# Five instead of four strips per head on VectorE, head sums on GpSimd, memory units later in the head

## The reference, cut to what matters

```python
scores = jnp.einsum('bsqhd,bthd->bqhst', qh, kh) * scale
probs = jax.nn.softmax(scores, axis=-1)
a_dot = jnp.einsum('bqhst,bthd->bsqhd', probs, vh)
a_mem = sigma_q @ memory / (sigma_q @ memory_norm)
out = a_dot * (1.0 - w) + a_mem * w          # x = x + out
x_qdq = quantised_to_fp8(_layernorm(x))      # x = x + x_qdq @ w.T
```

## Time and profile before

| what | value |
|---|---|
| median of three runs | 1942.49 us |
| the profiled execution | 1942.58 us, span 1940.5 us |
| PE busy | 1863.9 us, 96% |
| PEld busy | 1162.0 us, 60% |
| DVE busy | 1409.9 us, 73% |
| ACT busy | 1833.6 us, 94% |
| POOL busy | 107.2 us, 6% |
| granted TensorE clock | 1.000 |
| chain that ended last | ACT 76%, PE 21%, issue 2%, DVE 1% |

### The profile page before, as it was taken

One profiled execution on the slowest core, in us unless ns is written; L12 is line 12 of the kernel. 1 busy time (PEld: TensorE's weight loads), 2 busy tenths in 40 slices (PEclk: granted clock), 3 DMA queues, 4 the chain that ended last, 5 costly groups with the idle time before them and its releaser, 6 DMA issues.

```text
span 1940.5 us, 115379 instructions
## 1 busy us (share of the span) xinstructions
PE 1863.9 (96%) x54988; PEld 1162.0 (60%) x54996; DVE 1409.9 (73%) x1833; ACT 1833.6 (94%) x1596; POOL 107.2 (6%) x150
## 2 busy tenths in 40 slices
PE   8999999999999999999999999999999999999998
PEld 7885555556565555555555555555655555555555
DVE  6675777777777777787777777777777777777755
ACT  5556999999999999999999999999999999999997
POOL 5541000000000000000000000000000000000000
PEclk9999999999999999999999999999999999999999
DMA  6654111121112211222112211212112211222111
GB/s 220 201 187 153 54 54 40 45 57 45 54 41 56 78 49 42 56 58 64 47 49 56 78 47 44 57 46 76 44 53 57 78 50 41 56 50 72 43 47 46
DMA packets 131327, 130.38 MB, mean 67 GB/s; under 512 B 30451, under 2 KB 106455, under 8 KB 130855
## 3 DMA queue, kind: packets, MB, share of 16 engines
q1 hardware_dynamic: 129847, 121.15, 21.2%
q10 hardware_dynamic: 1008, 1.84, 0.3%
HBM read 86.96 MB, written 32.24 MB: 61 GB/s over the span
## 4 chain that ended last, share of the span: by engine, by line
ACT 76%; PE 21%; issue 2%; DVE 1%; POOL 0%; DMA 0%; ACTq 0%; DVEq 0%; POOLq 0%
ACT pool L865 74%; PE ps L1153 8%; PE ps L945 6%; PE ps L1028 4%; ACT pool L872 1%; PE ps L1200 1%; PE ps L918 1%; DMA resid<-in_x 0%; PE ps L984 0%; POOL q_sq L727 0%; PE ps L909 0%; POOL xn L704 0%; PE ps L926 0%; DVE v_tiles L1608 0%; DVE v_tiles L1610 0%
## 5 line engine op out<-in xcount | busy, mean ns | idle before, releaser
L865 ACT ACTIVATE pool<-ps 128x1536 f32<-128x1536 f32 (+1 forms) x1388 | 1710.1, 1413 | 17.0 <-PE ps L1028 14.7
L1153 PE MATMUL ps<-pool,v_st 64*32 64x128 f32 (+2 forms) x35744 | 1398.3, 357 | 14.7 <-issue 13.7
L1153 PEld LDWEIGHTS ps<-pool,v_st 64*32 64x32 f32 x35744 | 854.5, 106 | 210.0 <-issue 54.3
L1028 PE MATMUL ps<-q_st,k_st 51*32 51x512 f16 x16128 | 903.6, 381 | 49.0 <-ACT pool L865 11.6
L1028 PEld LDWEIGHTS ps<-q_st,k_st 51*32 51x32 f16 x16128 | 246.0, 89 | 474.3 <-ACT pool L865 427.5
L1593 DVE TENSOR_SCALAR late<-ps 128x512 int32<-128x512 f32 x248 | 171.6, 692 | 212.5 <-PE ps L1028 212.5
L1608 DVE SCALAR_TENSOR_TENSOR v_tiles<-late 128x2048 f32<-128x2048 f32 x62 | 142.1, 2293 | 148.1 <-PE ps L1153 144.7
L1612 DVE SCALAR_TENSOR_TENSOR pool<-v_tiles,late 128x2048 f32<-128x2048 f32 x62 | 142.1, 2292 | 2.1
L1610 DVE SCALAR_TENSOR_TENSOR v_tiles<-v_tiles,late 128x2048 f32<-128x2048 f32 x62 | 142.1, 2292 | 2.1
L1603 DVE SCALAR_TENSOR_TENSOR late<-late 128x2048 f32<-128x2048 f32 x62 | 141.6, 2285 | 0.0
L747 POOL TENSOR_TENSOR rstd<-var_eps,minus_half 128x1 f32<-128x1 f32 x32 | 23.0, 720 | 1696.8 <-DVE var_eps L1672 1696.8
(11 more groups left out here) (169 smaller groups left out, 955.1 us busy)
## 6 DMA issues: line engine op xcount, KB each, us to landing
v_st<-v_aug SPq DMA_DIRECT2D x64, 256.0 KB, 3.5
q_st<-q_aug SPq DMA_DIRECT2D x127, 128.0 KB
k_st<-k_aug SPq DMA_DIRECT2D x127, 128.0 KB
sigma_kept<-y_out SPq DMA_DIRECT2D x32, 256.0 KB, 2.0
q_aug<-parts SPq DMA_DIRECT2D x32, 256.0 KB, 2.7
wqT<-sigma_kept SPq DMA_DIRECT2D x32, 256.0 KB, 3.8
q_st<-q_aug SPq DMA_DIRECT2D x127, 64.0 KB
k_st<-k_aug SPq DMA_DIRECT2D x127, 64.0 KB
```

Of the source, the lines that this page charges most:

```text
L865: act.activation(probs[:, u % HELD, 0:UNITS[u].width * CH], scored(u).rearrange("p a b -> p (a b)"), ACT.Exp, bias=LIFT, scale=EXP_UNIT / ...
L1028: return pe.matmul(ps[VW * c:VW * c + VW, bank, :], k_st[RT * r:RT * r + AUG, n % 2, keys:keys + VW], q_st[RT * r:RT * r + AUG, n % 2, q * ...
L1153: last = pe.matmul(acc[r][VW * c:VW * c + VW, :].rearrange("v (i s) -> v i s", s=VW)[:, places, :], v_st[rows, n % 2, j, :], by_place[rows ...
```

## The change

Each of the heads 1 to 62 gets a fifth late strip, the last strip of the key tile before the last. ScalarE keeps 22 units per head, with one 3-wide unit fewer and one 2-wide more. In the even head the two memory units move from places 0 and 2 to 3 and 5. The late strips are weighed as a piece of four and a piece of one, in units 15 and 16 of even heads and 13 and 14 of odd ones. The polynomial is worked out in place in the pool, and its last step (`finish_late`) moves to the next head: first in even heads, behind the output of the tile in odd ones. Two of the four steps that join a head's sums move to GpSimd, except where the head before was the last of its chunk. The third strip's row tile alternates with every unit. Head 0 has 25 units for the same 64 strips, 24 before.

```diff
+LATE_STRIPS = tuple(range(HEAD_STRIPS - QG, HEAD_STRIPS)) + (HEAD_STRIPS - QG - 1,)
+LATE = len(LATE_STRIPS)
-UNITS_OF_HEAD = (["2memory", "3", "2memory"] + ["3"] * 7 + ["2late"] * 4 + ["3"] * 8,
-                 ["3", "3", "2product", "3", "2spare", "3", "3"] + ["2late"] * 4 + ["3"] * 11)
+EVEN_HEAD = ["3", "3", "3", "2memory", "3", "2memory"] + ["3"] * 3 + ["2late"] * LATE + ["3"] * 8
+ODD_HEAD = ["3", "3", "2product", "3", "2spare", "3", "3"] + ["2late"] * LATE + ["3"] * 10
-WEIGHED_LATER = ((0, 1, 2), (0, 1, 2, 3, 9))
-WEIGH_LATE_AT = 14
+WEIGHED_LATER = ((0, 1, 2), (0, 1, 2, 3))
+LATE_PIECES = ((0, 4), (4, 1))
+WEIGH_LATE_AT = (15, 13)
...
+            for n in range(1, LAST_HEAD):
...
+                if n % 2 == 0 and n >= HEADS:
+                    tile = (n - HEADS) // 2
+                    pool_e.wait_ge(f_eps, tile + 1)
+                    pool_e.tensor_tensor(rstd[:, 0, 0:1], var_eps[:, 0:1], minus_half[:, 0:1], ALU.pow).then_inc(f_rstd, 1)
+                    pool_e.wait_ge(f_rstd, tile + 1)
+                if n % HEADS != 0:
+                    add_sums(n - 1)
...
-                    last = strip_scores(THIRD_BANK[u % SLOTS], n, strip, (c // 2 + u // 2) % ROW_TILES, c)
+                    last = strip_scores(THIRD_BANK[u % SLOTS], n, strip, (c // 2 + u) % ROW_TILES, c)
...
+            def finish_late(n):
+                dve.wait_ge(late_step, n * CHAIN_STEPS)
+                dve.scalar_tensor_tensor(late_probs, late_probs, POWER[3], late_x, ALU.add, ALU.mult).then_inc(late_ready, 1)
...
             def head(n):
                 g, h = divmod(n, HEADS)
-                if n % 2 == 0:
-                    add_memory(n)
+                if n % 2 == 0 and n > 0:
+                    finish_late(n)
                 if n > 0:
                     take_sums(n - 1)
+                for unit in extras(n, "product", "weight") * (n % 2):
...
                 if n % 2 == 0:
+                    if n > 0:
+                        dve.wait_ge(sums_added, n - 1)
+                    add_memory(n)
                     add_memory(n + 1)
+                else:
+                    finish_late(n)
                 if n > 0:
-                    add_sums(n - 1)
+                    sum_halves(n - 1)
+                    if h == 0:
+                        add_sums(n - 1)
```

More of the change, by code:

```diff
@@ L99, in extra_of, with forms_of_head @@
     return None, 0
+def forms_of_head(n):
+    if n == 0:
+        return ["2"] * EARLY_UNITS + EVEN_HEAD[:-1] + ["2", "2"]
+    return (EVEN_HEAD, ODD_HEAD)[n % 2]
 def units_of(n):
     units, strip, names = [], 0, []
-    for form in ["2"] * EARLY_UNITS * (n == 0) + UNITS_OF_HEAD[n % 2]:
+    for form in forms_of_head(n):
         width, name = int(form[0]), form[1:]
@@ L748, in rstd_of_tiles, with add_sums @@
                     pool_e.wait_ge(f_rstd, i + 1)
[L750 to L755, removed]
+            def add_sums(n):
+                g, h = divmod(n, HEADS)
+                pool_e.wait_ge(rden_ready, n + 1)
+                pool_e.tensor_tensor(head_out[:, :, :, 0:DH], head_out[:, :, :, 0:DH],
+                                     rden[:, :, :].unsqueeze(3).to_broadcast([P, QG, TPC, DH]), ALU.mult)\
+                    .then_inc(head_out_ready, 1)
+                pool_e.wait_ge(head_out_ready, n + 1)
+                cols = resid[:, g * TPC:(g + 1) * TPC, :].rearrange("p t (q f) -> p q t f", q=QG)[:, :, :, h * DH:(h + 1) * DH]
+                pool_e.tensor_tensor(cols, cols, head_out[:, :, :, 0:DH], ALU.add).then_inc(sums_added, 1)
+            for n in range(1, LAST_HEAD):
+                if n == LAST_HEAD - 1:
+                    pool_e.wait_ge(scores_ready, EXP_BASE[LAST_HEAD - 1])
+                    pool_e.memset(q_st[:, 1, :].bitcast(F32), 0.0).then_inc(last_cleared, 1)
+                    pool_e.wait_ge(last_cleared, 1)
+                if n % 2 == 0 and n >= HEADS:
[5 more added lines that the diff above has]
+                    add_sums(n - 1)
+            rstd_of_tiles((NG - 1) * TPC, NT)
             pool_e.wait_ge(xq_ready, NT)
@@ L1174, in weigh_unit, with weigh_late @@
                     last.then_inc(pv_done, 1)
-            def weigh_late(n, x):
+            def weigh_late(n, piece):
+                first, strips = LATE_PIECES[piece]
                 pe.wait_ge(late_ready, n)
-                last = weigh(n, LATE_TILE, late_probs[:, x * CH:x * CH + CH], x, 1)
-                if x == LATE - 1:
+                j, q = divmod(LATE_STRIPS[first], QG)
+                last = weigh(n, j, late_probs[:, first * CH:(first + strips) * CH], q, strips)
+                if piece == len(LATE_PIECES) - 1:
                     last.then_inc(late_weighed, 1)
@@ L1233, in head @@
                         weigh_unit(weighed)
-                    x = u - EXP_BASE[n] - WEIGH_LATE_AT
-                    if n > 0 and 0 <= x < LATE:
-                        weigh_late(n, x)
+                    piece = u - EXP_BASE[n] - WEIGH_LATE_AT[n % 2]
+                    if n > 0 and 0 <= piece < len(LATE_PIECES):
+                        weigh_late(n, piece)
             def last_slot_free(i):
@@ L1594, in take_late, with late_powers @@
                                   -2.0 ** 23 / OCTAVE, LOWEST, ALU.mult, ALU.min).then_inc(late_taken, 1)
-            def chain_begin(step, width):
-                fixed, part = late_x[:, 0:width], late_z[:, 0:width]
+            def late_powers(step):
+                fixed, part = late_x, late_z
                 dve.tensor_scalar(part.bitcast(I32), fixed.bitcast(I32), MANTISSA, QUARTER,
@@ L1619, in late_exponentials @@
                 dve.wait_ge(late_taken, n * LATE)
[L1620 to L1624, removed]
+                late_powers((n - 1) * CHAIN_STEPS)
+                if n > 1:
                     dve.wait_ge(late_weighed, n - 1)
-                chain_end((n - 1) * CHAIN_STEPS, LATE * CH, late_probs).then_inc(late_ready, 1)
+                late_polynomial((n - 1) * CHAIN_STEPS)
+            def finish_late(n):
+                dve.wait_ge(late_step, n * CHAIN_STEPS)
+                dve.scalar_tensor_tensor(late_probs, late_probs, POWER[3], late_x, ALU.add, ALU.mult).then_inc(late_ready, 1)
             def take_sums(n):
@@ L1646, in add_sums @@
                 cols = resid[:, g * TPC:(g + 1) * TPC, :].rearrange("p t (q f) -> p q t f", q=QG)[:, :, :, h * DH:(h + 1) * DH]
-                dve.tensor_tensor(cols, cols, head_out[:, :, :, 0:DH], ALU.add)
+                dve.tensor_tensor(cols, cols, head_out[:, :, :, 0:DH], ALU.add).then_inc(sums_added, 1)
             def add_last_tile(t):
@@ L1751, in head @@
                         decode_weight(h // 2)
-                for unit in extras(n, "product", "weight"):
-                    if unit.extra == "product":
+                if n == LAST_HEAD - 1:
+                    for unit in extras(n, "product"):
                         ffn_out(*divmod(unit.number, TPC))
-                    else:
-                        copy_ffn_weight(unit.number)
                 if n + 1 < LAST_HEAD:
```

32 lines of the change are left out of this document (18 added, 14 removed).

## The result

The changed kernel takes 1977.24 us, the median of four runs (1973.80 to 1978.81), beside 1942.51 us for the kernel before: 1.0174 times as long, with an interval of 1.0157 to 1.0192. The forecast was 1975. The profiled execution's span grew from 1940.5 to 1977.1 us; it is the longest of the four, 1.6 us above their median.

What follows compares the result with a forecast made beforehand. ScalarE's pace was taken to set the time. From the profiled execution: 1942.6 - 26.5 + 0.1 + 26.0 + 15.4 + 6.6 + 11.2 = 1975 us, with a range from 1940 to 1994.

Steps and rivals of the forecast that it cites:

- What ScalarE saves: Heads 1 to 62 each trade a 3-wide unit for a 2-wide one on ScalarE: 62 x 0.428 = 26.5 us less.
- Unit 6: Even heads from 2 on: TensorE, late after unit 5's products and five strips, stalls ScalarE 0.84 us; +26.0 us.
- Rival 3: Units 6 and 12: scores run beside the weighing's tail, ScalarE stays unbroken; 1916 us, with half of it 1930; chance 0.12.
- Unit 12: Even heads with rounding: VectorE takes the first late strip only at 15.5 us, so ScalarE stalls; +33.2 us in all.
- VectorE's own sums in 7 heads: Even heads n = 8, 16 to 56: VectorE keeps both last sum steps on the path; 7 x 0.94 = +6.6 us.
- GpSimd's hindrance: GpSimd's sums run while VectorE rounds and slow it: 0.56 us in each of 20 heads, +11.2 us.
- The common part: Even heads 8 to 60: stall of 0.47 us at unit 12 and 0.10 at unit 14; 27 x 0.57 = +15.4 us.
- Odd heads at nothing: Odd heads: fewer weighing pieces cost nothing, ScalarE covers strips with 0.77 us of idle loads, VectorE keeps room; no loss.
- Chunk 0: Even heads of chunk 0: shorter path without moments, no gap ahead of unit 12, pair period near 54.1 us.
- The polynomial: VectorE's steps over 2560 columns: first two grow from 1.23 to 1.53 us, four others from 2.29 to 2.87.
- The port: GpSimd's sums beside VectorE's rounding: bounds nothing or 1.28 us per head in 20 heads; the skill makes full price likely.
- rival 1: VectorE waits in full for both GpSimd sum steps, 20 x 0.72 us more, 1990 us; chance 0.20.

Runs made afterwards that it cites:

- sums behind the rounding: Changed kernel with GpSimd's two sum steps held back in even heads with rounding until the rounding is done; 1960.21 us, 1.0112 times the kernel before.
- the control: The changed kernel unaltered, run again on one of the experiments' chips; 1975.62 us, 1.0181 times the kernel before.
- weighing at 15 only: Changed kernel with the late strips of odd heads weighed at units 15 and 16 instead of 13 and 14; 1965.62 us, 1.0131 times the kernel before.
- memory early, sums first: Changed kernel with memory units back at places 0 and 2 of even heads, VectorE's order left as changed; 1985.53 us, 1.0242 times the kernel before.

## Why the prediction was right, by its steps

- **What ScalarE saves** held: 64 wide units fewer and 65 narrow ones more in the by-shape rows, at the forecast's prices 65 x 0.915 - 64 x 1.343 = -26.5 us, at the measured intervals -26.2.
- **Unit 6.** Forecast 0.84 us, measured 0.86 with the forecast's prices and 0.90 from one start to the next, the same in 30 of 31 heads (1.55 in the other). The kernel after shows TensorE at that place: the products at unit 5, five strips weighed, and unit 6's scores behind them.

```profile
958.28 0.65 PE L1227 MATMUL ps<-mem_aug,wqT 128*32 128x129 f32 x16
958.85 1.36 PE L1178 MATMUL ps<-pool,v_st 64*32 64x256 f32 x48
959.96 0.48 PE L1053 MATMUL ps<-q_st,k_st 51*32 51x512 f16 x8
```

  From 958.85 to 959.96 are 1.11 us where I took 5 x 0.213 + 0.04 = 1.11. Rival 3, on which a faster result rested, asked for scores beside the tail of the weighing; it did not happen here either.
- **Unit 12.** Forecast 33.2 us, measured 29.1, with the parts not all right. VectorE's own sums in 7 heads: 0.94 forecast, and 1.24 less the 0.31 that is common, 0.93, measured. GpSimd's hindrance: 0.56 taken between 0 and 1.28, measured 0.71. The common part: 0.57 taken, about 0.31 measured, by the 0.21 us gap that "sums behind the rounding" leaves. The errors, +3 us from the one and -7 from the other, partly cancel; the path itself is right, and what was mis-sized is the sum of some fifteen durations that ends at 15.5 us, by a quarter of a microsecond. The 0.10 us of it that was to be lost at unit 14 is not lost there. That TensorE waits for L1593 (now L1620) in unit 11 came as said:

```profile
967.32 0.40 PE L1053 MATMUL ps<-q_st,k_st 51*32 51x512 f16 x4 [0.96 <-DVE late L1620]
```

- **Odd heads at nothing** is the step that failed. I had written that fewer weighing pieces cost nothing and had counted strips in full only in the units where I had seen the cover go. The four strips in one piece are 4 x 0.213 = 0.85 us more for TensorE at odd unit 13, where the idle loads that were to cover them are 0.77 us. Ahead of odd units 12 to 17 ScalarE loses 26.0 us (26.5 in the control, 19 to 21 in the five variants with the same odd heads) where it lost 11.9, and "weighing at 15 only" brings that to 9.6. That the odd heads' total rose by only 3.9 us is due to some 10 us less at their other units, which I had not named either and no run explains; in the five variants the total even lies 0.3 to 2.4 us below the kernel before. The prediction had itself named gaps in odd heads as a sign of being wrong. It came within 3 us because this and the too dear unit 12 have opposite signs: the two even terms are shown, the closeness of the total is partly luck.
- **Chunk 0.** I let it fit, with a period of 54.1 us. Three pairs there take (400.15 - 236.16) / 3 = 54.66, and later ones (1914.11 - 400.15) / 27 = 56.07. No even unit 12 stalls in chunk 0, as said; the half microsecond over is mostly odd heads again.
- **The polynomial** was taken as in proportion to its columns, 1.53 and 2.87 us; it took 1.494 and 2.826.
- **The port.** By the Trainium skill (SBUF — State Buffer, Who interferes with whom) the engine that holds the shared port pair keeps the other out for a whole instruction. By GpSimd's two durations that would make up to 1.36 us here, an estimate and rival 1's case; the rows show 0.70, half of it, and the second GpSimd step lengthened from 0.69 to 0.75 us. A hindrance is confirmed, its full price is not, and the measurement decides.

**What lies behind the odd gaps, and what stays open.** By the list, odd unit 13 stands to its narrow units as even unit 15 does, and ScalarE runs through even unit 15 without a gap. So the piece of four does not stall by its length alone. The delay in odd heads differs from head to head, 0.2 to 2.6 us, and TensorE's rows show waits named "issue" ahead of it, for nothing that the profile names. One such place in the kernel after: TensorE's weight loads, ScalarE's gap at odd unit 14 behind them, and two of the queues from 880 to 882.5 us (packets, MB, share of 16 engines):

```profile
883.33 0.59 PEld L1178 LDWEIGHTS ps<-pool,v_st 64*32 64x32 f32 x38 [0.63 <-issue]
```

```profile
885.28 1.45 ACT L890 ACTIVATE pool<-ps 128x1536 f32<-128x1536 f32 x1 [0.51 <-PE ps L1053]
```

```profile
q1 hardware_dynamic: 817, 0.91, 102.8%
q8 instruction: 1, 0.02, 2.5%
```

The kernel before has waits of this kind too. Ahead of its weighing loads, in the stretch of the earlier trace rows, and in the same stretch of the kernel after:

```profile
PEld ps L1153 <- issue: 53.3, 114, 2.6
```

```profile
PEld ps L1178 <- issue: 36.2, 105, 2.3
```

Every gap of ScalarE from odd unit 12 on, 26 in the kernel after, 18 before and 5 in "weighing at 15 only", has at least 0.4 us of such waits in the 4.5 us ahead of it; of the units there without a gap about one in three has any in the kernel after. Between odd units 10 and 17 they add up to 30.7 us in 50 places in the kernel after, 23.0 in 29 before and 12.0 in 18 in "weighing at 15 only", but between even units 12 and 19 only to 5.4 in 17. So even unit 15 is spared because few of them fall there, and later weighing in odd heads took away waits as well as giving room.

The traces' packets tell what they are. Queue q8, "instruction", brings 16 KB in each packet, 419 of them in the kernel after. All 27 issue waits of 0.5 us or more in its heads ended 1.3 to 1.6 us after such a packet had landed (34 of 35 in the kernel before, 1.1 to 1.8 us), where a moment taken at random lies anywhere from 0.4 to 4 us behind one. (Waits of some 0.5 us in even heads, behind the memory products of the kernel before and of those with early memory units, are of another kind.) The reading that fits is that TensorE stands until its next stretch of program code is there. In the 2 us ahead of the seven waits over 1 us the DMA engines were busy 40 to 105%; whether that load is what makes the code late was not separated, as no run moved the operand loads. Why GpSimd's 1.36 us cost VectorE only 0.70 is also open.

## What to carry to other kernels

When units of work are moved in a schedule in which two engines hand each other buffers, list for each engine how late it may be at every unit, wide or narrow, and add up every unit's work against that room, not only those that the change names; here a product moved by three units cost twice what the relief of the bounding engine gained. A helper engine that takes work off a path can give most of it back if it runs beside that same path: put it behind the stretch that matters. Move the producer and the reader together: the early units pay only with the early reading. And where an engine has no room, small waits that cost nothing elsewhere reach the engine that sets the pace.

## What was not expected of the hardware

In "memory early, sums first" TensorE pauses in each even head, its weight loads for 2.56 us and its matmuls for 1.96. One such pause is shown here by windows (from the left: window, its length, busy us of PE, PEld, DVE, ACT and POOL, the granted clock, DMA share, GB/s):

```profile
957.00:959.00 2.00, 0.89 (x32) 0.64 (x40) 1.19 (x5) 0.69 (x1) 0.00 (x0) 1.00 0.45 105
959.00:961.00 2.00, 2.00 (x64) 1.35 (x56) 1.84 (x5) 1.65 (x2) 0.00 (x0) 0.64 0.47 138
961.00:963.00 2.00, 2.00 (x63) 1.62 (x51) 1.38 (x5) 1.74 (x2) 1.33 (x2) 0.51 0.03 8
963.00:965.00 2.00, 2.00 (x97) 1.89 (x89) 1.90 (x4) 1.51 (x2) 0.76 (x2) 1.00 0.00 0
```

The granted clock fell from 1.00 (2.4 GHz) to 0.50 (1.2 GHz) 1.5 us after the pause had ended, and was back at 1.00 by 963. This came in 11 of the 30 even heads from 232 to 1858 us, 0.2 to 1.5 us behind the pause; in the other 19 the same pause of 2.56 us left the clock at 1.00. In the 11 ScalarE's gaps within 15 us of the pause add up to 2.34 us, in the 19 to 1.67: 11 x 0.68 = 7.5 us, which is what carries that run from the middle of what was expected to its upper end. In the kernel after, thirteen pauses of the weight loads of 1.5 to 3.3 us were followed by no fall, and in the kernel before three of 1.9 to 2.6 us by none; in the control, where three reach 2.4 us, one was. So in a loop like this a pause of TensorE costs its length, and sometimes another 0.7 us for the clock that follows; when it does and when not, these rows do not tell.
